# Layer 1's first batch of rows, loaded and normed from expert 7's third block on

## The reference

```python
x = x + jnp.tanh(g_xattn[0]) * _L0_xattn_ref(_layernorm(x, axis=-1), ctx_1024, ...)
x = x + jnp.tanh(g_ffn[0]) * _L0_ffn_ref(_layernorm(x, axis=-1), L0_ffn_router_w, L0_ffn_up_w, L0_ffn_down_w)
x = x + jnp.tanh(g_xattn[1]) * _L1_xattn_ref(_layernorm(x, axis=-1), ctx_1024, L1_xattn_Wq, ...)
x = x + jnp.tanh(g_ffn[1]) * _L1_ffn_ref(_layernorm(x, axis=-1), L1_ffn_gate_w, ...)
```

```python
scores = jnp.einsum('bqc,bkc->bqk', queries, keys) * scale
attn = jax.nn.softmax(scores, axis=-1)
```

## Time and profile before

| | |
|---|---|
| timed runs | median 1534.33 us (1529.26 to 1537.96, 3 runs) |
| the profiled execution | 1531.72 us, its span 1529.9 us |
| mean granted TensorE clock | 0.946 |
| busy in the span | PE 1376.3 us (90%), DVE 790.2 (52%), ACT 737.8 (48%), POOL 504.6 (33%) |
| end of layer 0's experts, start of layer 1's attention | 929 to 963 us of the span |
| scatters into the residual in layer 0 | 56 by `list_i`, 16 by `m_i_last` |

### The profile page before, as it was taken

How to read it: one execution, slowest core, us unless ns; L and a number is a source line. 1 busy time by engine, 2 the same in 40 slices (tenths; PEclk the granted TensorE clock), 3 DMA queues, 4 the chain that set the end, 5 groups by cost and what they waited for, 6 DMA issues and landing times. The chain is left out here.

```text
span 1529.9 us, 25592 instructions
## 1 busy us (share of the span) xinstructions
PE 1376.3 (90%) x9908; PEld 1272.7 (83%) x9908; DVE 790.2 (52%) x1658; ACT 737.8 (48%) x1399; POOL 504.6 (33%) x389
## 2 busy tenths in 40 slices
PE   5799989989985999999999995999888859999997
PEld 5686866966854999999999995899888849999997
DVE  3645666666556453554454232455756685456421
ACT  3344544443444465555565452354443444566553
POOL 1200100100001664655665442121211106767643
PEclk9899999999997999999999998899998979999998
DMA  4302022021013453553553224011210236555322
GB/s 134 117 11 75 33 72 73 15 85 59 21 64 91 132 145 51 145 147 64 119 152 61 51 41 126 1 51 66 97 48 28 70 97 212 136 133 158 65 51 37
DMA packets 73676, 127.51 MB, mean 83 GB/s; under 512 B 7952, under 2 KB 53664, under 8 KB 73504
## 3 DMA queue, kind: packets, MB, share of 16 engines
q1 hardware_dynamic: 46816, 81.92, 16.3%
q0 software_dynamic: 26688, 43.34, 14.8%
HBM read 100.44 MB, written 24.79 MB: 82 GB/s over the span
## 5 line engine op out<-in xcount | busy, mean ns | idle before, releaser
L2384 DVE TENSOR_TENSOR m_hidden_lo<-m_act_out,m_hidden_hi 128x512 fp32r<-128x512 f32 x224 | 155.1, 693 | 357.9 <-ACT m_hidden_hi L2326 347.3
L411 PE MATMUL banks<-m_down_hi,m_hidden_hi 128*128 128x256 f32 x896 | 258.5, 288 | 1.5 <-DVE m_hidden_lo L2384 1.0
L411 PE MATMUL banks<-m_down_lo,m_hidden_hi 128*128 128x256 f32 x896 | 256.1, 286 | 2.6 <-issue 2.6
L411 PE MATMUL banks<-m_down_hi,m_hidden_lo 128*128 128x256 f32 x896 | 255.8, 285 | 0.0
L411 PE MATMUL banks<-m_xt_hi,m_up_hi 128*128 128x256 f32 x640 | 184.2, 288 | 1.4 <-DVE m_xt_lo L2367 1.4
L411 PE MATMUL banks<-m_xt_hi,m_up_lo 128*128 128x256 f32 x640 | 180.7, 282 | 0.0
L411 PE MATMUL banks<-m_xt_lo,m_up_hi 128*128 128x256 f32 x640 | 180.6, 282 | 0.0
L411 PEld LDWEIGHTS banks<-m_down_hi,m_hidden_hi 128*128 128x128 f32 x896 | 172.3, 192 | 4.5 <-DVE m_hidden_lo L2384 1.2
L411 PEld LDWEIGHTS banks<-m_down_lo,m_hidden_hi 128*128 128x128 f32 x896 | 172.3, 192 | 3.0 <-issue 3.0
L411 PEld LDWEIGHTS banks<-m_down_hi,m_hidden_lo 128*128 128x128 f32 x896 | 172.2, 192 | 0.0
L2463 POOL DMA_INDIRECT m_other_block<-rows,list_i x84 | 91.5, 1089 | 164.5 <-DVE list_i L1468 102.3
(11 more groups left out here) (365 smaller groups left out, 3542.5 us busy)
## 6 DMA issues: line engine op xcount, KB each, us to landing
stage<-in_down SPq DMA_DIRECT2D x22, 512.0 KB, 4.9
stage<-in_ctx_cols SPq DMA_DIRECT2D x26, 402.0 KB, 3.6
stage<-in_ctx_rows SPq DMA_DIRECT2D x20, 512.0 KB, 3.8
stage<-in_up SPq DMA_DIRECT2D x20, 512.0 KB, 5.2
m_stage<-in_up SPq DMA_DIRECT2D x11, 512.0 KB, 4.3
m_stage<-in_down SPq DMA_DIRECT2D x10, 512.0 KB, 4.0
rows<-xn SPq DMA_DIRECT2D x8, 528.0 KB, 3.9
stage<-in_ctx_picked SPq DMA_DIRECT2D x8, 512.0 KB, 5.5
```

The costliest lines, as they stand in the source:

```text
L411: mm = q.e.matmul(dst, a, b, start=first and n == 0, stop=last and n == 2, skip_group_check=True)
L2384: q.e.tensor_tensor(lo, m.act[(n * HP + h) % ACTS], f32(hi), ALU.subtract).then_inc(*hidden_lo.mark((layer, n, h)))
```

## The change

It does four things.

1. A semaphore `first_rows`. GpSimd raises it in layer 0 at the start of expert 7's block 3, behind the wait for the scatters begun so far, those of blocks 0 and 1 among them. A list rises with the token, so what stands at 512 or later in it lies in a later batch than the first; blocks 2 and on of expert 7 touch nothing of batch 0. `sync_x` of batch 0 in layer 1 waits for `first_rows` instead of "all". If there is no block 3 (j <= 3 at the finish), it is raised behind "all".
2. GpSimd's power for batch 0 goes from the start of `gpsimd_attention_1` into the new `gpsimd_finish`, ahead of the last scatter if expert 7 had more than three blocks, behind it otherwise. Since this depends on the number of blocks, the finish now stands in each end of the nested `If`s of expert 7 (`either`), once for each number of blocks from 1 to 8.
3. The tiles of layer 1's attention are laid out in another order: `stage` ahead of `x_in`, `x0` next to it, then `bv_wide`, `x1`, `x2` and `mixed`, with `x3` last, so that `x0` lies on memory of weights that expert 6 had used.
4. `scalar_turn_x` of batch 0 waits for the last products up instead of "all", and `scalar_mix` of batch 0 waits for "all".

```diff
@@ attention_memory
             if layer == 1:
                 m.r = pair(n + "routed", [P, KD, TOK], st)
+                m.stage = [sb(n + f"stage{i}", [P, STAGE], F32, st)[:, :] for i in range(2)]
+
                 m.xin = sb(n + "x_in", [P, TT, D], F32, st)
-                m.stage = [sb(n + f"stage{i}", [P, STAGE], F32, st)[:, :] for i in range(2)]
+                m.x = [sb(n + "x0", [P, TT, D], F32, st)]
                 m.bv_wide = pair(n + "bv_wide", [P, KD, P], st)
+
+                m.x += [sb(n + f"x{i}", [P, TT, D], F32, st) for i in (1, 2)]
+                m.mixed = [sb(n + f"mixed{i}", [P, D], F32, st) for i in range(2)]
...
-            m.x = [sb(n + f"x{i}", [P, TT, D], F32, st) for i in range(4 if layer else 2)]
+                m.x = [sb(n + f"x{i}", [P, TT, D], F32, st) for i in range(2)]
+            else:
+                m.x.append(sb(n + "x3", [P, TT, D], F32, st))
@@ sync_x
-            if layer:
+            if layer and b:
                 q.wait_ge(*added.of(0, "all"))
+            elif layer:
+                q.wait_ge(first_rows.sem, 1)
@@ scalar_turn_x
                 q.wait_ge(*projected.of("o", 1, b - 2, 1))
-                q.wait_ge(*added.of(0, "all"))
+                q.wait_ge(*up_done.of(0, E * NB - 1, HP - 1))
@@ scalar_mix
+            if layer and b == 0:
+                q.wait_ge(*added.of(0, "all"))
@@ gpsimd_attention_1
-            gpsimd_power(q, "in", 1, 0)
+            powers.mark()
+            powers.mark()
             gpsimd_power(q, "in", 1, 1)
@@ further
+        def further(q, layer, held, own, e, j, block, finish):
 
             if j == NB:
+                either(q, layer, j, finish)
                 return
             before_, passed = [s.count for s in own], dict(q.passed)
             with q.e.If(held > BLOCK * j):
                 block(q, layer, e, j)
-                further(q, layer, held, own, e, j + 1, block)
+                further(q, layer, held, own, e, j + 1, block, finish)
             with q.e.Else():
                 catch_up(q, own, before_)
+                either(q, layer, j, finish)
@@ gpsimd_block
             if j != 1:
                 gpsimd_added(q, layer, n - 2)
+            if (layer, e, j) == (0, E - 1, 3):
+                q.e.nop().then_inc(*first_rows.mark())
@@ gpsimd_experts
-                blocks(q, layer, own, e, gpsimd_block)
+                blocks(q, layer, own, e, gpsimd_block, gpsimd_finish if e == E - 1 else None)
+            added.mark()
+            added.mark((layer, "all"))
+
+        def gpsimd_finish(q, layer, j):
+
             gpsimd_added(q, layer, E * NB - 2)
             for there, begun in zip(other_in, others_begun):
                 q.e.wait_ge(there.sem, q.e.snap(begun))
                 q.e.nop().then_inc(*rested.mark())
+            if layer == 0 and j > 3:
+                gpsimd_power(q, "in", 1, 0)
             gpsimd_add(q, layer, E, 0)
             gpsimd_added(q, layer, "all")
+            if layer == 0 and j <= 3:
+                q.e.nop().then_inc(first_rows.sem, 1)
+                gpsimd_power(q, "in", 1, 0)
```

More of the change, by code:

```diff
@@ L213, in build @@
         rested = signal("rested")
+        first_rows = signal("first_rows")
         small = sb("small", [P, NCOL])
@@ L305, in attention_memory @@
             m.pt = [pair(n + f"probs_t{i}", [P, TOK], st) for i in range(3)] + [pair(n + "probs_t_tail", [P, P], st)]
-            m.mixed = [sb(n + f"mixed{i}", [P, D], F32, st) for i in range(2)]
             if layer == 0:
+                m.mixed = [sb(n + f"mixed{i}", [P, D], F32, st) for i in range(2)]
                 m.row = sb(n + "row", [4, TOK + P], F32R, st)
@@ L2148, in catch_up, with blocks @@
                     q.e.nop().then_inc(s.sem, s.count - n)
-        def blocks(q, layer, own, e, block):
+        def blocks(q, layer, own, e, block, finish=None):
             held = count_of(q, layer, e)
@@ L2153, in blocks @@
                 block(q, layer, 0, 1)
-            further(q, layer, held, own, e, always(e) + 1, block)
-        def further(q, layer, held, own, e, j, block):
+            further(q, layer, held, own, e, always(e) + 1, block, finish)
+        def further(q, layer, held, own, e, j, block, finish):
             if j == NB:
+                either(q, layer, j, finish)
                 return
@@ L2162, in further, with either @@
                 block(q, layer, e, j)
-                further(q, layer, held, own, e, j + 1, block)
+                further(q, layer, held, own, e, j + 1, block, finish)
             with q.e.Else():
                 catch_up(q, own, before_)
+                either(q, layer, j, finish)
             q.passed = passed
+        def either(q, layer, j, finish):
+            if finish is not None:
+                counts, passed = [s.count for s in signals], dict(q.passed)
+                finish(q, layer, j)
+                q.passed = passed
+                for s, n in zip(signals, counts):
+                    s.count = n
         up_ring = Ring([ps[:, i, :] for i in range(5)])
```

## The result

The changed kernel takes 1524.41 us in the median of nine runs (1513.27 to 1528.63), the kernel before 1534.33 (1529.26 to 1537.96): ratio 0.9926, 95% interval 0.9898 to 0.9954. By this ratio, in which all runs count, it is 11.3 us less, between 7 and 16; the two medians alone lie 9.9 us apart. It is faster, as forecast, but by two thirds of the 16.8 us of the sum, and the median lies above the stated range, which ended at 1522.

The account below looks back on a forecast made before the run. TensorE's 13.35 us rest between the layers, an uncovered chain of latencies, was taken as the bound. Terms of 14.4 and 2.4 us summed to 16.8 less, giving 1514.9 or 1517.5; forecast 1516 us, range 1510 to 1522.

Parts of the forecast that it names:

- the sum: Where the layers meet: 14.4 us from earlier projections plus 2.4 us from the high clock, 16.8 us less.
- The condition: Expert 7 of layer 0 runs five blocks, 0 to 4, so the finish with the early power is run.
- the load: SyncE's load of batch 0 for layer 1 moves from 941.05 to about 907, landed by 917, cost-free.
- VectorE's measure: Measuring batch 0's rows comes behind VectorE's last low part, from about 930.5 to 932.7, in idle time.
- GpSimd's power: Batch 0's power runs ahead of the last add, done at 934.1 with 1 us to spare, costing nothing.
- The projections start at 941.26 instead of 955.66: 14.4 us: At layer 1's start, earlier normed rows and transposes let TensorE's projections begin 14.4 us sooner.
- 1.6 is nearer to the first, so I take the high clock: The 1.6 us rest before the projections leaves the clock high, as one of 1.49 us did: 2.4 us more.
- my first rival: The clock falls all the same in the 1.6 us rest: gain 14.4 us, time 1518.4, chance 0.18.
- What is late next: In layer 1, x1's load is in time for VectorE, cost 0 (bound 1.5 us); the 2.19 us rest comes earlier.
- The second (late steps): VectorE's and GpSimd's small steps come up to 1.1 us late, so the clock falls: gain 13.3, time 1519.5, chance 0.11.
- The third: The change does nothing, through too few blocks in expert 7 or a held load: 1531.7 to 1534.3, chance 0.05.
- the fourth: Slower if x0 lands past 946.2, since the last add waits behind it: for example 13.8 us, 1545.5; chance 0.01.

Follow-up runs that it names:

- e4: Changed kernel with the second half of batch 0's transposes in the bank of the mix: 1519.03 us, ratio 0.9913 to the kernel before.
- e5: Changed kernel with the fold's columns in the mix's bank, the fold right behind the last products down, and own banks for both transpose groups: 1521.02 us, ratio 0.9888.
- e6: e5 with 12 needless transposes behind the real ones, filling TensorE's rest: 1524.04 us, ratio 0.9925 to the kernel before.
- e7: Changed kernel with 19 needless transposes in TensorE's two short rests: 1520.01 us, ratio 0.9891; run again with more timed executions, ratio 0.9922.
- e8: Kernel before with 105 needless transposes in its long rest and 7 and 12 in the two rests behind: ratio 0.9996.
- e9: The kernel of e6 again, with more timed executions: median 1516.24 us, ratio 0.9921 to the kernel before.
- c1: Changed kernel once more without an edit, for a second trace: 1522.83 us, ratio 0.9929 to the kernel before.
- c3: Changed kernel without an edit, with more timed executions: 1516.31 us against 1528.51 for the kernel before beside it, ratio 0.9919.

## Why the prediction was wrong in size

**What bounds.** Right: the rest of 13.35 us was a bare chain of latencies, and the change takes it away.

**The condition** (five blocks, so the early copy runs), **the load** at 907, **VectorE's measure** and **GpSimd's power**: right. This trace reaches the place 1.0 us later than that of before. With this added, the sum has VectorE at 931.5 and the power done at 935.1; VectorE began at 932.02, 0.5 us after its last low part, and the power was done at 935.53. Nothing waited for it, since ScalarE was busy with `m_y` until 936.0.

**"The projections start at 941.26 instead of 955.66: 14.4 us"** failed in a step that I had not looked at: banks. Matmuls write their results to banks, and three banks are used in turn here. The fold holds two of them and the first four transposes take the third, so the second four must wait until VectorE has subtracted the fold (`a_weights_lo`). In the kernel before, ScalarE evicted the fold only at 951.77, behind the normed rows, and VectorE was through with it at 953.07. The first four transposes began at 951.92 and took until then at the low clock, so the wait was hidden. The projections started 7.76 us behind the last `m_y` instead of 6.96, so the term is 13.6 us, 0.8 less. e4 gave it a bank and won 0.87 at the projections.

**"1.6 is nearer to the first, so I take the high clock", 2.4 us**, failed. The clock fell in each of three traces of the changed kernel, and also in e4 and e5, where 1.65 us was the only rest behind the transposes. With the rests filled it stayed at 1.00 in five traces of five (e6, e7 twice, e8, e9). The size of the term was right: e7 got 2.7 us and 2.4 us by filling the rests. What failed is not only the guess but its measure, the length of the rest. In e8 a rest of 2.39 us brought no fall, and behind the rest of 2.2 us before the first `a_probs`, which every trace has, both outcomes occur in one and the same kernel. By TensorE's timelines, the changed kernel's first trace runs all 13 transposes there at the low clock:

```profile
959.36 3.18 PE L942 MATMUL banks<-small,a_probs 128*65 128x128 f32 x13 [2.18 <-ACT a_probs L921]
```

And in c1 the same transposes run at the high clock:

```profile
957.02 0.76 PE L942 MATMUL banks<-small,a_probs 128*65 128x128 f32 x5 [2.19 <-ACT a_probs L921]
958.23 1.10 PE L942 MATMUL banks<-small,a_probs 128*128 128x128 f32 x8 [0.45 <-DVE a_weights_lo L549]
```

So one row of a stretch with 1.49 us of rest and clock 1.00 could not decide it. The fall was my first rival, at 0.18; it should have been the likeliest case. Its gain, with the bank's 0.8 us off, is 13.6 us, just what the traces show.

**The sum** is thus 13.6 and not 16.8 us, and 1531.72 - 13.6 = 1518.1 for the profiled execution, 1520.7 from the median. The measured 11.3, 10.9 and 12.4 us are compatible with it, though all three lie below. The remaining 3.7 us up to 1524.41 are thus within the scatter, and I can show no place that gives anything back; that nothing does is not shown.

**What is late next**: right. x1 was in time: VectorE's idle time before the first maximum is 1.71 us as before. The rest of 2.2 us comes as before, only earlier; its fall came in the first trace and in c3, and not in c1.

**Rivals.** The second (late steps) cost nothing: VectorE began 0.5 us late, but ScalarE has no idle time ahead of the normed rows. The third and the fourth are refuted by the load at 906.59. **The range** was too narrow above: it took 1519.5 as the dearest likely case and 3 us for scatter, while layer 1's experts alone scatter by 8 us, so that by my estimate a median of a few runs may be 2 to 4 us off. Two traces of one kernel would have told that; one can't.

The Trainium skill, in TensorE: Matmul & The Clock Gate (section on the HAM clock gate), says that the activity window is free-running, so the cold stretch varies with its phase. At the place itself the clock fell in all five traces of the changed kernel, e4 and e5, so the alternation that the rival drew from this was not seen. But the moment does vary: from the second transposes on in c1, from the projections on in the other two of the changed kernel. Farther on it fits, as at the rest of 2.2 us above and in e6 and e9, which are one kernel: its attention took 264.93 us in one execution and 269.81 in the other.

## What to carry to other kernels

A rest of TensorE that stands behind a chain of small steps was worth its whole length here (13.35 us, and 13.6 won). But before it is added up, list what each step that now comes sooner needs beside its data: here a bank that the fold still held. A short rest that is left counts with a fall of the clock until several rows say otherwise, and its length alone doesn't settle it: price both outcomes. And before a term of 2 to 5 us is hunted by times, look at how much the other stages scatter in two traces of the same kernel: here it was 8 us, and only the distance between two marks in the trace, steady to 0.3 us, told the variants apart.

## What the runs showed of the hardware that was not expected

Layer 1's experts take between 281.5 and 289.5 us in fourteen traces with the same instructions on TensorE, VectorE and ScalarE. Part of it goes with the clock: over this stage the five traces of more than 287 us were granted 0.93 or 0.94, the nine shorter ones 0.95. Part of it is there at the start of the stage. In the first trace of before ScalarE's `m_xt_hi` is released by TensorE after 10.49 us, in the changed kernel's after 12.33 us by something that the profile calls remote and that no engine's row explains, 1.8 us more. ScalarE's timeline of the kernel before:

```profile
1271.69 0.60 ACT L2299 ACTIVATE m_xt_hi<-banks 128x512 fp32r<-128x512 f32 x1 [10.49 <-PE banks L2205]
```

And of the changed kernel:

```profile
1260.65 0.60 ACT L2324 ACTIVATE m_xt_hi<-banks 128x512 fp32r<-128x512 f32 x1 [12.33 <-remote]
```

And filling a rest of TensorE with needless transposes kept the clock at 1.00 wherever it was tried (e6, e7, e8, e9), for 12 to 124 instructions that nobody waits for; that it doesn't show in the times says how little 2.5 us are in a kernel of 1530.
